# One block of Wq per batch, and the last rotary stores four steps later

## What is computed

```python
x = layernorm(x + self_attention(x, w_qkv, w_o))     # 32 heads on 8 kv heads, rotary, causal
x = layernorm(x + cross_attention(x, ctx, Wq, bq, Wk, bk))
x = layernorm(x + ffn(x))                            # weights decoded from 4 bit planes and a table
```

## Time and profile before

| | us |
|---|---|
| median of 3 runs | 1242.52 (1241.6 to 1245.41) |
| the profiled execution | 1240.88 |
| its span | 1239.0 |
| TensorE busy | 1219.4 (98%) |
| VectorE busy | 859.5 |
| GpSimd busy | 617.6 |
| ScalarE busy | 579.6 |

### The profile page before, as it was taken

How to read it: one execution, slowest core, us unless ns; L and a number is a source line. 1 busy time by engine, 2 the same in 40 slices (tenths; PEclk the granted TensorE clock), 3 DMA queues, 4 the chain that set the end, 5 groups by cost and what they waited for, 6 DMA issues and landing times.

```text
span 1239.0 us, 23600 instructions
## 1 busy us (share of the span) xinstructions
PE 1219.4 (98%) x8134; PEld 1037.4 (84%) x8134; DVE 859.5 (69%) x2483; ACT 579.6 (47%) x1659; POOL 617.6 (50%) x522
## 2 busy tenths in 40 slices
PE   8999999999999999999999999999999999999997
PEld 6888889999778888888887887888888888888886
DVE  7999989666878888788776973354362634866564
ACT  5131212547877877878860222342342424743332
POOL 3522122357866776776750000454556354985552
PEclk9999999999999999999999999999999999999999
DMA  8254535455775535535533113327243365623211
GB/s 291 71 192 135 172 122 181 145 175 153 199 209 150 142 112 156 144 105 159 146 108 122 51 39 110 145 68 265 67 162 118 120 221 182 224 79 145 98 73 68
DMA packets 130870, 174.12 MB, mean 141 GB/s; under 512 B 36672, under 2 KB 91968, under 8 KB 130112
## 3 DMA queue, kind: packets, MB, share of 16 engines
q1 hardware_dynamic: 130752, 172.62, 44.0%
HBM read 115.94 MB, written 56.62 MB: 139 GB/s over the span
## 4 chain that ended last, share of the span: by engine, by line
PE 91%; DMA 3%; POOL 2%; ACT 1%; DVE 1%; SPq 1%; issue 1%; POOLq 0%; DVEq 0%; ACTq 0%
PE bank L799 14%; PE bank L801 14%; PE bank L800 14%; PE bank L993 12%; PE bank L927 6%; PE bank L885 5%; PE bank L912 4%; PE bank L1241 4%; PE bank L1239 4%; PE bank L1240 4%; PE bank L850 3%; PE bank L958 2%; PE bank L808 2%; DMA vv<-v_scr 1%; PE bank L962 1%; PE bank L881 1%
## 5 line engine op out<-in xcount | busy, mean ns | idle before, releaser
L2249 POOL TENSOR_TENSOR prob<-prob,rinv 128x512 f32<-128x512 f32 x192 | 206.4, 1077 | 136.8 <-DVE rinv L1806 136.3
L1361 ACT ACTIVATE prob<-bank,nmax 128x256 f32<-128x256 f32 (+1 forms) x512 | 211.7, 430 | 68.3 <-DVE nmax L1798 68.2
L1798 DVE CUSTOM_DVE_ANT_0 bank<-bank,mask 128x256 f32<-128x256 f32 (+1 forms) x512 | 170.4, 385 | 30.2 <-issue 21.1
L927 PE MATMUL bank<-ident,prob 128*128 128x128 f32 x768 | 115.2, 273 | 2.7 <-POOL prob L2249 2.7
L927 PEld LDWEIGHTS bank<-ident,prob 128*128 128x128 f32 x768 | 93.9, 140 | 27.2 <-POOL prob L2249 5.4
L1361 ACT ACTIVATION_READ_ACCUMULATOR prob<-bank,nmax 128x1 f32 x512 | 109.9, 215 | 0.0
L1962 DVE SCALAR_TENSOR_TENSOR k_lo<-bank,bA,k_hi 128x512 fp32r<-128x512 f32 x32 | 24.0, 751 | 122.5 <-ACT k_hi L1497 121.1
L912 PE MATMUL bank<-k,q 96*128 96x256 f32 (+1 forms) x512 | 103.4, 304 | 1.8 <-DMA vv<-v_scr 1.8
L993 PE MATMUL bank<-wo_hi,att_hi 128*128 128x512 f32 x256 | 103.7, 405 | 0.3 <-DVE y L1844 0.2
L993 PE MATMUL bank<-wo_hi,att_lo 128*128 128x512 f32 x256 | 101.4, 396 | 0.0
L799 PE MATMUL bank<-cT_hi,m_hi 128*128 128x512 f32 x256 | 100.4, 392 | 0.7 <-DVE cT_lo L1661 0.7
(11 more groups left out here) (223 smaller groups left out, 3297.0 us busy)
## 6 DMA issues: line engine op xcount, KB each, us to landing
q<-qk_scr SPq DMA_DIRECT2D x192, 128.0 KB, 2.9
x_st<-x_scr SPq DMA_DIRECT2D x32, 512.0 KB, 4.1
qk_scr<-rot SPq DMA_DIRECT2D x60, 256.0 KB, 2.6
xc_in<-x_cols SPq DMA_DIRECT2D x32, 256.0 KB, 4.9
y<-x SPq DMA_DIRECT2D x16, 512.0 KB, 5.0
x_scr<-y SPq DMA_DIRECT2D x16, 512.0 KB, 3.0
cx_in<-ctx_in SPq DMA_DIRECT2D x16, 512.0 KB, 4.8
x_scr<-x_st SPq DMA_DIRECT2D x16, 512.0 KB, 3.2
```

The lines of the kernel that those rows point to most:

```text
L927: mm = nc.tensor.transpose(tb[:, at * P:(at + 1) * P], prob[:, k % 4, c:c + P], ident[:, :])
L1361: mm = nc.scalar.activation(prob[:, k % 4, i * keys:(i + 1) * keys], SBANK[pos][:, i * keys:(i + 1) * keys], ACT.Exp, bias=nmax[:, k % 4, ...
L1798: mm = nc.vector.tensor_tensor_reduce(part, part, mask[:, 2 * P - keys:2 * P], 1.0, BIGGEST, ALU.add, ALU.min, nmax[:, k % 4, i:i + 1])
L2249: nc.gpsimd.tensor_tensor(pr, pr, rinv[:, k % 4, 0:n].unsqueeze(2).to_broadcast([P, n, keys]), ALU.mult)\
```

## The change

The low parts of items 10 and 11 move on GpSimd from steps 3 and 5 to steps 7 and 9 of the second batch. In SyncE's order y1's first load and head 5's load go in front of these items' stores, with a wait for the turned items (r_ready) ahead of them. Wq's blocks 1 to 7 are no longer loaded in the second batch: batch b loads block b behind its last head, with a wait for the blocks before. ScalarE waits for the blocks so far, and for all of them behind the last batch. The steps at which ScalarE splits Wq are as before, and block 0's load stays behind the stores of item 11.

```diff
@@ SyncE, stage2_batch @@
                 if age == 1:
                     load_unit(b, 4)
+                    sp.wait_ge(r_ready, LAST_PAIRS)
+                    load_y1(0, 0)
+                    load_unit(b, 5)
                     store_item(10)
                     store_item(11)
                     load_wq((0,))
                     for slot in range(2):
                         sp.wait_ge(r_stored[slot], 64 * ((LAST_PAIRS + 1 - slot) // 2))
                     sp.wait_ge(v_stored, 32 * GROUPS)
-                    load_y1(0, 0)
...
-                for unit in range(5, KVH):
+                for unit in range(6 if age == 1 else 5, KVH):
                     load_unit(b, unit)
-                    if age == 1:
-                        load_wq(range(2 * unit - 9, min(2 * unit - 7, KT)))
+                wait(sp, wq_ld, 16 * (b - 1))
+                load_wq((b,))
                 store_x1(b - 1, 0)
                 if not last:
                     load_unit(b + 1, 0)
-                if age == 1:
-                    load_wq((7,))
                 load_y1(b, 0)
@@ ScalarE @@
                         if age == 1:
                             act.wait_ge(wq_first_ld, 16)
                         else:
-                            act.wait_ge(wq_ld, 16 * (KT - 1))
+                            act.wait_ge(wq_ld, 16 * (b - 1))
                         wq_high(b - 1, WQ_HIGH_STEP[k])
...
+            act.wait_ge(wq_ld, 16 * (KT - 1))
             for half in range(2):
                 wq_high(KT - 1, half)
@@ GpSimd, stage2_batch @@
-                    if age == 1 and k in (3, 5):
-                        rope_low(item_pair(10 + k // 5))
+                    if age == 1 and k in (7, 9):
+                        rope_low(item_pair(10 + k // 9))
                     if age and k in WQ_LOW_STEP:
                         wq_low(b - 1, WQ_LOW_STEP[k])
```

## The result

| | before | changed | ratio |
|---|---|---|---|
| median, us (8 runs each) | 1241.62 | 1247.03 | 1.0046 (1.0036 to 1.0056) |
| profiled execution, us | 1240.88 | 1248.92 | |
| span of it, us | 1239.0 | 1247.0 | |

The kernel became 5.4 us slower. Where, is seen best by the starts of the score groups on TensorE (L912), 24 a batch, in both traces.

What follows compares the result with a forecast made beforehand. The prediction took TensorE to bound the kernel (91% of the chain), so a change pays only where it stands still. 7.1 + 2.0 - 2.8 = +6.3 us gave 1248.8 us from a 1242.52 us median; range 1244.5 to 1252.5.

Steps and rivals of the forecast that it cites:

- transposes of group 10, at full clock: TensorE, second batch: these transposes wait for ScalarE's copy and come at 338.7 in place of 331.6, +7.1 us.
- slow clock until them: TensorE, from step 13's scores to group 10's transposes: half speed makes 1.25 us into 2.5, transposes 0.5 us later.
- slow clock behind them: TensorE after group 10's transposes, until 342.2: 3.0 us at half speed do 1.5 us of work, +1.5 us.
- Part 1: Low parts moved on GpSimd: VectorE's Wo split no longer overlaps one, so steps 6 to 9 come 0.45 us earlier.
- Part 2: Wq's first block, queued behind item 11's stores, lands at 335.2; ScalarE waits at step 9, TensorE stops: +7.1 us.
- Part 3: TensorE's clock falls to 1.2 GHz in the 6.8 us stop, half speed until 342.2: +2.0 us, between 0 and 2.8.
- Part 4: Second and third batch: seven Wq blocks leave, head 5 loads ahead of the stores, TensorE's head waits go: -2.8 us.
- Part 5: Later batches: one Wq block each, loaded where SyncE stands still in the third batch, costs zero.
- (b): TensorE's stop comes but its clock does not fall, or too late to matter: +4.3 us, 1246.8 us; chance 0.18.
- (d): ScalarE does not wait at step 9's split, the block landing by 326.4 us: -3.3 us, 1239.3 us; chance 0.12.
- (c): Wq's first block lands after 9.1 us because it meets other transfers: +11.9 us, 1254.4 us; chance 0.08.
- (e): Second batch keeps its DMA waits since the stop only shifts the loads: +9 us, 1251.6 us; chance 0.10.

Runs made afterwards that it cites:

- the low parts alone: The kernel before with only the low parts of items 10 and 11 moved to steps 7 and 9: 1250.55 us, ratio 1.0068.
- block 0 first: The changed kernel with the load of Wq's block 0 in front of the stores of items 10 and 11: ratio 0.9980, and 0.9986 when repeated.
- TensorE kept busy: The changed kernel with 26 unused matmuls ahead of the scores of step 13 of the second batch: 1247.50 us, ratio 1.0050.
- the split at 11: The changed kernel with ScalarE's first split of Wq at step 11 in place of 9, GpSimd's subtraction at 12 in place of 10: ratio 1.0026.
- block 0 behind head 6: The changed kernel with the load of Wq's block 0 moved behind head 6's load: 1252.86 us in one run.
- the low parts back: The changed kernel with the low parts of items 10 and 11 back at steps 3 and 5: 1240.96 us, ratio 0.9991.

## Why the prediction was right, point by point

Forecast +6.3 us, measured +5.4 us for the whole and +4.76 us for stage 2, on which the sum was made. The forecast time, 1248.8 us, started from the 1242.52 us of three runs; eight have 1241.62, so 0.9 us of its 1.8 us of error is the start's. That the whole is nearer to the forecast than stage 2 is luck: the 0.7 us between them come from no term of the sum. Its terms:

| term | forecast, us | measured, us |
|---|---|---|
| TensorE before the stop | -0.45 | -0.65 |
| transposes of group 10, at full clock | +7.1 | +6.8 |
| slow clock until them | +0.5 | +0.5 |
| slow clock behind them | +1.5 | +0.4 |
| head waits | -2.8 | -2.9 |
| a block per batch | 0 | 0 |

(6.8: the copy of group 8's transposes ends at 338.17 + 0.62 = 338.79, less the 0.41 us of the start and less 331.60. 0.5: 339.27 less 338.79. 0.4: from 339.27 - 0.41 - 331.60 = 7.26 to the 7.66 of step 14.)

The granted clock (third from last) of the kernel before at its start, where the earlier trace rows have the first matmuls:

```profile
6.00:7.00 1.00, 1.00 (x3) 0.81 (x3) 0.00 (x0) 0.24 (x1) 0.00 (x0) 1.00 1.03 345
```

- **Part 1 was right**, the mechanism with it: GpSimd's earlier time is worth little, and what is gained comes from the two instructions that no longer lie on each other. It was undersized by 0.2 us, since the split alone takes 1.23 us and not the 1.43 us of its twin, which itself lay beside the scaling of step 7. The runs with the low parts at 3 and 5 show that the gain is 0.65 us against one outcome of that meeting and 1.35 us against the other.
- **Part 2 was right** to 0.3 us: item 11's low part ended at 330.0 (forecast 329.85), the block was issued at 331.9 (331.7) and ScalarE split it at 335.4 (335.2); with the 0.41 us of the start taken off, each is some 0.25 us earlier than forecast. Undoing the low parts' steps, or taking the block out from behind the stores, removes the stop; moving the low parts alone brings it.
- **Part 3 had the sign and the mechanism, and its second term was three to four times too large.** The slow work lasted 3.1 us (336.96 to about 340.1), not the 5.5 us of the kernel's start. The step that failed is the use of the earlier trace rows as a duration that begins when work comes back. In the runs here the clock was low from its fall on, for 6.8 us after stops of 3.1, 6.6 and 6.7 us and for 13.7 us after one of 12.3 us, and what was left of that for work was 5.9, 3.1, 4.7 and 5.4 us. It fell 2.2 to 4.5 us after the last matmul, not at the 4.9 us of the earlier trace rows. Nor do show that the first twelve matmuls ran at the low level: the granted clock reads 1.00 there (the line above), and only their distance, 0.43 us where later ones have 0.23 us, is that of the slow stretch here.
- **Part 4 had the right size and a wrong reason for this kernel.** With the low parts alone the head waits go as well. What the spread blocks and head 5's load bring is 2.9 us only where there is no stop, as in block 0 first.
- **Part 5 was right**: the later batches did not change.
- **The rivals.** (b), the clock doesn't fall, forecast +4.3 us; the fall is there but its price nearly as small. (d), ScalarE does not wait, would have given -3.3 us; the kernel with block 0 first is this case, with -3.5 us in stage 2, but only -2.6 and -1.6 us in the whole. (c), a landing of 9.1 us, and (e), the head waits stay, did not happen.

The 0.7 us between stage 2 and the ratio of the whole are within what executions differ by (1246.1 to 1248.92). What decides in an execution whether the last fold has its 1.6 us of slow clock, and why the fold of Wk started 1.0 to 1.15 us later in three of the profiled executions (the changed kernel, the low parts alone, TensorE kept busy), stays open.

## What to carry to other kernels

When a step is moved later, follow everything that is queued behind its products: here a subtraction of 1.4 us moved by four steps made a store late, the store stood in front of a load in the one DMA queue, and a third engine had its wait for that load in the middle of its critical work. The load had no need of the store; putting it ahead cost nothing that the trace shows and turned the loss into a gain. A transfer's wait that is hidden by a stop elsewhere is not a gain of the change, and it comes back when the stop is mended unless its own cause is gone.

## What the runs showed of the hardware

- TensorE's clock went from 2.4 to 1.2 GHz 2.2 us after its last matmul with the split at 11, 2.9 us in the changed kernel, 4.1 us with block 0 behind head 6, 4.5 us with the low parts alone, and 4.9 us at the end of the kernel before. A stop of 3.1 us was enough for it.
- The price of the slow clock did not follow the stop's length. The stops of 3.1 and 6.6 us had slow stretches of the same 6.8 us, and 0.9 us and 3.7 us of these lay in the stop; the first cost 2.4 us, the second 0.5 to 0.9 us.
- The clock also fell to 0.50 for 3.4 us with TensorE busy throughout, in seven of the twelve profiled executions: in six behind the four matmuls of two rows in the last fold (L1055), in one, with the split at 11, behind sixteen of two rows (L1105) and sixteen short ones. It cost 1.6 us, and five executions that ran the same matmuls didn't have it.
- A VectorE subtraction of two SBUF operands and a GpSimd one lengthen each other, and which of the two pays is not the same in each kernel: 1.88 and 1.71 us before, 2.57 and 0.73 us with the low parts back, for what takes 1.23 and 0.72 us alone. The Trainium skill, "SBUF — State Buffer", section "Who interferes with whom", says that a VectorE instruction with two SBUF inputs contends with a GpSimd instruction that reads SBUF, and that the order of issue decides who blocks. The traces agree that they contend. As for the order, I read it from the lengths: 2.57 us is about 1.23 us and the two halves of the low part (0.73 us each), as if VectorE had waited for both, and with 1.88 and 1.71 us it seems to have got in between them. What made the order change isn't shown.
